# Two chunks' first FFN and first maximum blocks of layer two inside the first attention, tanh SiLU, row-product modulation

## The reference, cut to what matters

```python
x = L0_attn_x
mod = (_silu(L0_c) @ L0_wmod).reshape(1, 6, 1, -1)
sa, ca, ga, sb, cb, gb = (mod[:, i] for i in range(6))
ga = (2 * (ga >= 0) - 1) * jnp.maximum(jnp.abs(ga), 0.25)      # gb likewise
h = _layernorm(x) * (1 + ca) + sa
x = x + ga * attention0(h)      # causal, 16 heads of 16, softmax((K.Q)*0.25 - distance)
h = _layernorm(x) * (1 + cb) + sb
x = x + gb * ffn0(h)            # (silu(h Wg^T * gs) * (h Wu^T * us)) Wd^T * ds, inner 704
# layer two: the same with its own mod; attention without mask, 16 heads of 16;
# FFN: shared expert of 352 + the best two of 8 experts of 176 for each token
```

## Time and profile before

| | us |
|---|---|
| median of 3 runs | 1543.2 |
| lowest, highest | 1535.55, 1543.47 |
| the profiled execution | 1535.36 |
| its span, first to last instruction | 1533.5 |
| TensorE busy | 1399.3 |
| VectorE busy | 1182.8 |
| ScalarE busy | 1038.1 |
| GpSimd busy | 343.9 |

### The profile page before, as it was taken

One profiled execution on the slowest core, in us unless ns is written; L12 is line 12 of the kernel. 1 busy time (PEld: TensorE's weight loads), 2 busy tenths in 40 slices (PEclk: granted clock), 3 DMA queues, 4 the chain that ended last, 5 costly groups with the idle time before them and its releaser, 6 DMA issues. The chain is left out here.

```text
span 1533.5 us, 35240 instructions
## 1 busy us (share of the span) xinstructions
PE 1399.3 (91%) x13320; PEld 591.2 (39%) x13320; DVE 1182.8 (77%) x1528; ACT 1038.1 (68%) x2052; POOL 343.9 (22%) x472
## 2 busy tenths in 40 slices
PE   6988898999899998986999999999999999999988
PEld 5543333333333354441333333333333333247665
DVE  5687897898885044888999979997999789617665
ACT  2345676777788841231899979998999889964432
POOL 2501131200100041223140038201300040145234
PEclk9999999999999998996999999999999999999999
DMA  7821120011000003222100200000000000013454
GB/s 223 150 47 40 47 77 28 30 44 35 1 2 2 1 15 70 49 49 64 81 7 8 55 4 7 7 7 6 7 7 7 7 2 2 12 68 92 143 155 128
DMA packets 56867, 68.51 MB, mean 45 GB/s; under 512 B 9819, under 2 KB 52379, under 8 KB 55963
## 3 DMA queue, kind: packets, MB, share of 16 engines
q1 hardware_dynamic: 53635, 57.87, 14.3%
q0 software_dynamic: 3072, 8.39, 1.8%
HBM read 45.26 MB, written 26.74 MB: 47 GB/s over the span
## 5 line engine op out<-in xcount | busy, mean ns | idle before, releaser
L1800 DVE TENSOR_REDUCE mpart<-psum 128x2 f32<-128x1024 f32 (+2 forms) x832 | 913.2, 1156 | 102.7 <-PE psum L1232 84.1
L1535 ACT ACTIVATE probs<-psum 128x512 f32<-128x512 f32 (+3 forms) x1664 | 846.3, 573 | 163.5 <-PE psum L1263 89.7
L1288 PE MATMUL psum<-probs,v_region 128*17 128x256 f32 (+2 forms) x6144 | 491.6, 392 | 11.8 <-ACT out_sb L1550 8.0
L1232 PE MATMUL psum<-key_region,row_region 50*128 50x512 f16 (+3 forms) x1664 | 320.0, 377 | 61.0 <-DVE mpart L1800 45.1
L1263 PE MATMUL psum<-row_region,key_region 52*128 52x512 f16 (+3 forms) x1664 | 347.4, 376 | 18.2 <-ACT probs L1535 13.0
L1263 PEld LDWEIGHTS psum<-row_region,key_region 52*128 52x128 f16 x1664 | 97.4, 93 | 352.7 <-ACT probs L1535 289.8
L1288 PEld LDWEIGHTS psum<-probs,v_region 128*17 128x17 f32 x6144 | 102.6, 95 | 201.5 <-issue 99.1
L1232 PEld LDWEIGHTS psum<-key_region,row_region 50*128 50x128 f16 x1664 | 94.2, 93 | 165.2 <-DVE mpart L1800 96.5
L1034 POOL TENSOR_SCALAR mp<-mx 128x16 f16<-128x16 f32 x32 | 10.3, 321 | 651.3 <-DVE mx L1811 620.2
L1570 ACT ACTIVATE probs<-psum,gate_s 128x512 f32<-128x512 f32 (+1 forms) x24 | 16.4, 682 | 74.3 <-PE psum L1331 74.3
L1822 DVE SCALAR_TENSOR_TENSOR probs<-psum,up_s,probs 128x512 f32<-128x512 f32 (+1 forms) x24 | 17.9, 747 | 52.7 <-PE psum L1340 43.7
(11 more groups left out here) (192 smaller groups left out, 1326.2 us busy)
## 6 DMA issues: line engine op xcount, KB each, us to landing
parts<-key_region SPq DMA_DIRECT2D x32, 256.0 KB, 3.1
key_region<-parts SPq DMA_DIRECT2D x48, 128.0 KB, 4.4
sorted_x<-in_zero SPq DMA_DIRECT2D x46, 128.0 KB, 2.6
key_region<-sorted_x SPq DMA_DIRECT2D x46, 128.0 KB
sorted_y<-key_region SPq DMA_DIRECT2D x46, 128.0 KB
row_region<-parts SPq DMA_DIRECT2D x144, 32.0 KB
key_region<-in_wmod SPq DMA_DIRECT2D x2, 1536.0 KB, 11.6
x_sb<-in_x SPq DMA_DIRECT2D x4, 512.0 KB, 8.5
```

Source lines behind the costliest of these rows:

```text
L1232: mm = pe.matmul(bank(b + par)[:, 0:w], rows[at, g, hp, r * P:(r + 1) * P], keys[at, g * HP + hp, q * CH:q * CH + w], start=True, stop=not ...
L1288: mm = pe.matmul(psum[32 * h:32 * h + VW, SUM_BANK, lo:hi], v_sb[:, jt, g * HG + h, :], probs[:, (S0[y] + s) % 2, h, lo:hi], start=(jt == ...
L1535: nc.scalar.activation(probs[:, (S0[y] + s) % 2, 2 * hp + par, off:CH], psum[:, e % 3, off:CH], ACT.Exp, scale=SCALES[y]).then_inc(s_p, 1)
L1800: V.tensor_reduce(mpart[:, n % NG, at:at + 2, q:q + 1], psum[:, b:b + 2, 0:w], AX.X, ALU.max).then_inc(drained(*item)[0], 1)
```

## The change

The planner puts the FFN of chunk 0 and of chunk 1 into the first attention: the pairs of chunk 0 at steps 62, 65, ... 77, its down halves at 80 and 82, its second-layer norm at 84 to 86, its projections at 88 and 90; the pairs of chunk 1 at steps 135, 137, ... 145, its down halves at 147 and 149, its norm at 151 to 153, its key projection at 155. From step 138 on, each step also gets one max block of the second attention's first units (22 in all). Each of these FFN items and projections holds one of the attention's two PSUM slots until a new mark, `hf`, in the next step; in that time all else goes through the other slot. Three groups' keys and rows of the second layer are loaded in the last three units (`load_group`), as the first attention's unit has given its place up.

The SiLU of these two chunks is computed as x/2 (1 + tanh(x/2)): a Tanh on ScalarE and two `scalar_tensor_tensor` on VectorE in place of Silu and one. The FFN weights are split on GpSimd at unit 8 instead of unit 9. The middle stage keeps chunks 2 and 3, the values of all chunks, the query side of chunk 1, both sides of 2 and 3, and 60 max blocks. The modulation columns become eight products of 256 columns (four of them in four column groups of the array, 32 wide), a copy, and two transposes.

```diff
+LINES = (0, 1, 3, 4)
-        more = [("wf", 0, k - 1)] if n == 2 * NG + 1 and 1 <= k < 1 + 2 * KD else []
+        more = [("wf", 0, k - 1)] if n == 2 * NG and 1 <= k < 1 + 2 * KD else []
+FREE_STEP = 138
+EARLY = {0: (62, 3, 80, 88, 90), 1: (135, 2, 147, 155, None)}
...
+            extra = ([], [], []) if y else ffn_in_attention(n, k)
             out.append(("sc", y, s, n, k, 0))
-            out += work[:first]
+            out += extra[0] + work[:first]
...
             out.append(("sc", y, s, n, k, 1))
-            out += work[first:second]
+            out += extra[1] + work[first:second]
...
-            out += during_attention(y, n, k)
+            out += extra[2] + during_attention(y, n, k)
...
+def ffn_in_attention(n, k):
+    s = first_step(0, n) + k
+    out = [[], [], []]
+    for tc, (pair, every, down, keys, row) in EARLY.items():
+        for c in range(NC[0]):
+            if s == pair + every * c:
+                out[0].append(("hg", 0, tc, c))
+                out[1].append(("hid", 0, tc, c))
+            if s == pair + every * c + 1:
+                out[0] += [("hf",), ("hh", 0, tc, c)]
+        for z in range(2):
+            if s == down + 2 * z:
+                out[0].append(("dm", 0, tc, z))
+                out[1].append(("dn", 0, tc, z))
+                out[2].append((("sa", "st")[z], 2, tc))
+            if s == down + 2 * z + 1:
+                out[0].append(("hf",))
+        if s == down + 4:
+            out[2].append(("nm", 2, tc))
+        if s == down + 5:
+            out[1].append(("ln", 2, tc))
+        if s == down + 6:
+            out[0].append(("lh", 2, tc))
+        for side, at in [part for part in ((1, keys), (0, row)) if part[1]]:
+            if s == at:
+                out[0].append(("qk", 1, tc, side))
+                out[2].append(("ql", 1, tc, side))
+            if s == at + 1:
+                out[0].append(("hf",))
+    if n > NU - NG and k == 1:
+        out[2] += [("group", n - 1 - (NU - NG))]
+    free = s - FREE_STEP
+    if free >= 0:
+        out[1] += [b for m in range(NG - 1) for b in pairs_of(1, m) if b[5] == 0][free:free + 1]
+    return out
...
+    for c in range(NC[0]):
+        out.append(("hg", 0, 2, c))
+        out.extend(tail(0, c))
+        blocks(1 + (c > 1))
+        out.append(("hid", 0, 2, c))
+        if c == 1:
+            loaded[0] = 2
+        blocks(1 + (c > 1))
+        if c in (2, 4):
+            value(c // 2 - 1)
...
+                    if held is None:
+                        turn[family] = turn.get(family, -1) + 1
+                        b = family[turn[family] % len(family)]
+                    else:
+                        b = 1 - held
+                    if n == 1 and item[0] in ("hg", "dm", "qk"):
+                        held = b
...
+                elif item[0] == "hf":
+                    turn[0, 1] = held + 1
+                    held = None
...
+            def load_group(g):
+                sp.wait_ge(*parts_stored(1, 0, 1))
+                sp.wait_ge(*parts_stored(1, 0, 0))
+                sp.wait_ge(s_e, HG * first_step(0, NU - NG + g + 1))
...
-                for i in range(8):
-                    col = (0, 1, 3, 4)[i // 2] * D + (i % 2) * P
-                    for k in range(KD):
-                        mm = pe.matmul(bank(b)[:, i:i + 1], wmod[y][:, k, col:col + P],
-                                       cs[:, y * KD + k:y * KD + k + 1], start=(k == 0), stop=(k == KD - 1))
+                for k in range(KD):
+                    for j, part in enumerate(LINES):
+                        mm = pe.matmul(bank(b)[32 * j:32 * j + 32, 0:D], csb[:, y * KD + k, 0:32],
+                                       wmod[y][:, k, part * D:(part + 1) * D], start=(k == 0), stop=(k == KD - 1))
...
+                    mm = pe.transpose(bank(b)[:, c * P:(c + 1) * P], mod_lines[:, c * P:(c + 1) * P], ident[:, :])
...
+                if in_attention(y, tc):
+                    nc.scalar.activation(early_e[k % 2][0:f, :], psum[0:f, bank_of(("hid", y, tc, c)), :], ACT.Tanh,
+                                         scale=gate_h[0:f, c:c + 1]).then_inc(s_sil, 1)
+                    return
...
+                if in_attention(y, tc):
+                    e = early_e[k % 2][0:f, :]
+                    link(V.scalar_tensor_tensor(e, e, 1.0, psum[0:f, b, :], ALU.add, ALU.mult))
+                    ins = V.scalar_tensor_tensor(t, up, both_h[0:f, c:c + 1], e, ALU.mult, ALU.mult)
```

187 lines of the change are left out of this document (116 added, 71 removed).

## The result

The changed kernel takes 1582.6 us (median of 4 executions, 1578.2 to 1588.4) against 1539.4 for the kernel before; the ratio on record is 1.0275, with an interval of 1.0242 to 1.0308 (the quotient of the two medians is 1.028). I had forecast 1510. The profiled execution took 1578.2 us with a span of 1576.5, against 1535.4 and 1533.5.

What follows compares the result with a forecast made beforehand. Bounds differed by stretch: TensorE and VectorE full mid first attention, VectorE idle some 130 us later, VectorE narrowly bounding the second. Middle -62, first attention +52, second -17, prologue -3 gave -30: 1510 us given, range 1479 to 1539.

Steps and rivals of the forecast that it cites:

- I take 52: First attention: 52 us longer, between 38 and 80, with part of the 58.9 us of added products absorbed by gaps.
- The held slot: First attention, some 19 steps with one slot left: a block's matmul waits for the reduction before it, 6 to 11 us.
- Second attention, -17: Second attention: 30 fewer max blocks make it 17 us shorter, the middle between 0 and -34.
- Middle, -62: Middle stage, last score of first attention to first of second: 138 us instead of 200, 62 less; range -55 to -68.
- (b): Middle stage, chunk 3's six pairs with chunk 2's down halves and keys: 41 us.
- (a): Middle stage, chunk 2's six pairs with the first attention's tail, two value items and 22 max blocks: 39 us.
- (c): Middle stage, from chunk 3's first down product to the second attention's first score: 57 us.
- Prologue, -3: Prologue: eight 256-column products, a copy and two transposes take 3.8 us instead of 6.83, 3 us less (0 to -6).
- The weight split, nothing: GpSimd's FFN weight split one unit earlier costs nothing; some 3 us if its cover fails, beside a norm's root.
- Rival 1: First attention: held slot makes a chain, about 5 us more a held step; slower, 1548 up to 1556 us; chance 0.08.
- rival 3: Full price: nothing absorbed in the first attention (+68), second attention gains only 5; 1523 to 1531 us; chance 0.16.
- Rival 2: First attention: 24 table loads of 1.283 us, 31 us on ScalarE; 1533 to 1541 us; chance 0.05.

Runs made afterwards that it cites:

- half_reduce: The kernel before, with each VectorE maximum of the second attention taken over only the left half of its columns: 1505.8 us, ratio 0.9793.
- fewer_middle: The kernel before, with 11 max blocks moved from the middle into the second attention (471 instead of 460): 1549.4 us, ratio 1.0048.
- silu_in_attention: The changed kernel, with Silu and one VectorE product instead of Tanh and two in the two chunks inside the attention: 1575.9 us, ratio 1.0206.

## Why the prediction was wrong

It said faster by 30 us, and the kernel became slower by 43.

- **What bounds the kernel** held: three kinds of stretch, and VectorE idle for some 130 us. What I made of it didn't. VectorE's idle time is a gain only for work that is VectorE's; I filled it with work that is TensorE's, where TensorE was already 92 to 95% busy.
- **First attention, "I take 52"**: +96 by the table. This is the step that failed, 44 of the 73 us by which the sum was off. My upper end was 80. The half that said "22 blocks go into those gaps at about nothing" was right (2.8 us). The other half, that a part of the FFN goes there too, was wrong: matmuls that left at steps 135 to 147 gave back their full time (10.2 of 10.3 us), and chunk 1 cost 39.6 against its TensorE sum of 28.1. By the terms of the sum: the 58.9 us of products were to be cut by idle time and gaps; they were paid nearly in full, and on top came some 32 us (93.8 - 58.9 - 2.8), where the sum had 6 to 11 for the held slot and nothing for the clock. In the rows, TensorE's busy time grew by 20.2 us more than the 58.9 (79.1, in which the 22 blocks and the slower matmuls are), and its idle time by 14.5. The sign "steps 62 to 91 over 2.60 + 1.4 us each" came: 4.32 us.
- **The held slot, "6 to 11 us"**: I priced it as a matmul that waits for one reduction. The timeline shows a queue: the reduction stands behind both products of the holder, and the score products of the next step behind the block. How much of the 32 us that is, no run isolates: emptying those steps of blocks was worth some 7 or 8 us net of what the blocks cost elsewhere, a shorter chain on VectorE (Silu) at least 4.6, and the two don't add. The waits of TensorE's matmuls for VectorE were 12.1 us in chunk 0's stretch, 6.8 of them for reductions, where the same steps before had 3.4; my sign of 15 us for reductions didn't come. The granted clock was 0.92 and 0.96 in these stretches, which I hadn't priced; before it was 1.00.
- **Second attention, -17**: -2.8. I took the middle of 0 and -34 for lack of a row that said which. half_reduce shows a ceiling of 17.4 us even for far more relief of VectorE, and fewer_middle that the kernel stood near the knee, where one block more costs 1.25 and one less some 0.1. The 0.2 us for each of 30 steps, 5 us in all, that I had worked out and then raised, was nearer.
- **Middle, -62**: -49.9. Part (b) came out as told; (a) and (c) took 5.5 and 7 us more, and the wait for keys returned.
- **Prologue, -3**: -3.4, by the step given. That four column groups run at a quarter of the time was right; the 3.69 us that I took for eight products were four, so the products took 1.94 instead of 0.9, and the copy and the transposes less than I had allowed. That the item came out at 3.4 against 3.8 is two errors that cancel.
- **The weight split, nothing**: 3.9 us; its price if uncovered, "some 3 us", was near, its mechanism (the norm's root) wrong.
- **Rival 1** named the sign and the decision point: 4.3 us on a held step. With the 93.8 us of both chunks over 19 held steps it is 4.9. But the waits that it describes are at most the 14.5 us of idle time that TensorE gained in both stretches; the greater part is **rival 3**, full price, which I had let end at +68 because it left the waits and the clock out. Each had a part of the mechanism, and I had added neither to the other.
- **Rival 2**, table loads: none occur, and where silu_in_attention forced 24 of them, they cost nothing.

What stays open: how the some 32 us beyond the products divide between the held slot's queue, the added work of VectorE and the clock; what made the clock fall; why the middle still takes 145 us with 28 blocks fewer; and where the repaired projections lose their time again.

## What to carry to other kernels

Work moved from one stage to another where TensorE is over 90% busy in both is a zero sum before any wait is counted: price its matmuls in full, and count as a gain only the idle time of TensorE that it fills (here 22 blocks of two 0.2 us matmuls cost 0.13 us each, and the groups of six at steps 135 to 147 their whole 1.29). Where an item holds one of two buffers over several engines' work, look for what stands in order behind it on each engine. Before you call a relief a gain, count what moved and where it went: the 17 us that left chunk 0's steps took 15 blocks with them. Where three engines are nearly full (96, 91 and 89% in the second attention), test the relief of one by taking far too much off it: that gives the ceiling, and it is small.

## What the runs showed of the hardware

- Eight float32 products of 256 columns in four column groups of 32 took 1.94 us, where four plain ones took 3.62: 0.24 against 0.9 us each, a quarter. The profile has two records for each of these products (16 and 8).
- A norm instruction pair on VectorE took 0.73 us alone and 1.93 beside a GpSimd product of 128x704. In the same place the granted clock was 0.50 for 10.3 us with the GpSimd split there, and 1.00 without it.
- 24 table loads of 1283 ns inside an attention cost nothing where ScalarE had been waiting for scores: the two stretches that hold them became 6.9 and 3.5 us shorter with one VectorE product less a pair, with the granted clock at 1.00 instead of 0.93.
